# Seven tiles for the transposed adjacency block, with four five-chunk groups rotating through five of them

## The reference, cut to what matters

```
n, d = x.shape                      # 3327, 128
h = Wq.shape[0] // d                # 8
q = (x @ Wq.T).reshape(d, n, h)     # 128 heads
a = jnp.einsum('dnh,dmh->dnm', q, k) * scale
a = a + spatial_encoding + edge_encoding      # both are adj
a = jax.nn.softmax(a, axis=2)
out = jnp.einsum('dnm,dmh->dnh', a, v)
```

## The kernel before, in words

| group | steps | kind | size |
|---|---|---|---|
| 0 | 0, 1, 2, 5, 6 | summing | 2080 KB |
| 1 | 3, 4, 8, 12, 13 | product | 2080 KB |
| 2 | 7, 9, 10, 11, 14 | summing | 2080 KB |
| 3 | 15, 16, 18, 19, 20 | summing | 2080 KB |
| 4 | 22, 23, 24 | summing | 1248 KB |
| 5 | 17, 21, 25 | product | 1248 KB |

## Time and profile before

### The profile page before, as it was taken

How to read it: one execution, slowest core, us unless ns; L and a number is a source line. 1 busy time by engine, 2 the same in 40 slices (tenths; PEclk the granted TensorE clock), 3 DMA queues, 4 the chain that set the end, 5 groups by cost and what they waited for, 6 DMA issues and landing times. The chain is left out here.

```text
span 10714.4 us, 541771 instructions
## 1 busy us (share of the span) xinstructions
PE 10354.1 (97%) x216536; PEld 6775.6 (63%) x216536; DVE 9602.2 (90%) x10333; ACT 10168.5 (95%) x7764; POOL 8419.5 (79%) x4247
## 2 busy tenths in 40 slices
PE   8859999999999999999999999999999999999998
PEld 6626666666666666666666666666666666666666
DVE  7789999999998999999998999999998999999997
ACT  4459999999999999999999999999999999999997
POOL 4448888888887888888887888888887888888885
PEclk9989999999999999999999999999999999999999
DMA  7681111111112111111112111111112111111113
GB/s 226 204 272 43 42 42 42 42 42 42 42 42 83 42 43 42 43 42 43 42 42 81 42 42 42 42 42 42 42 42 81 42 42 42 42 42 42 42 42 89
DMA packets 579045, 652.59 MB, mean 61 GB/s; under 512 B 168827, under 2 KB 517914, under 8 KB 573114
## 3 DMA queue, kind: packets, MB, share of 16 engines
q1 hardware_dynamic: 577209, 622.77, 21.4%
HBM read 485.17 MB, written 137.18 MB: 58 GB/s over the span
## 5 line engine op out<-in xcount | busy, mean ns | idle before, releaser
L1137 DVE SCALAR_TENSOR_TENSOR at_sum<-attention_adj_t,at_score 128x832 f32<-128x832 f32 x9216 | 8808.9, 1016 | 883.7 <-PE at_score L1079 793.6
L1059 POOL TENSOR_TENSOR at_single<-at_single,attention_adj_t 128x832 f32<-128x832 f32 x4096 | 8083.9, 1997 | 1804.1 <-ACT at_single L1154 1767.3
L1157 ACT ACTIVATE at_sum<-at_sum 128x2496 f32<-128x2496 f32 x3072 | 7352.0, 2393 | 10.7 <-DVE at_sum L1137 10.7
L1079 PE MATMUL at_score<-attention_q,attention_k 128*32 128x512 bf16 (+1 forms) x106496 | 7193.4, 346 | 141.0 <-DVE at_sum L1137 61.1
L1079 PEld LDWEIGHTS at_score<-attention_q,attention_k 128*32 128x32 bf16 x106496 | 3607.0, 144 | 2238.3 <-DVE at_sum L1137 772.3
L1095 PE MATMUL at_acc<-at_sum,attention_v 128*9 128x208 f32 x73728 | 4848.5, 339 | 3.7 <-issue 2.7
L1154 ACT ACTIVATE at_single<-at_score 128x832 f32<-128x832 f32 x4096 | 3716.9, 957 | 40.9 <-PE at_score L1079 38.9
L1095 PEld LDWEIGHTS at_acc<-at_sum,attention_v 128*9 128x9 f32 x73728 | 1876.7, 91 | 904.0 <-issue 6.7
L1095 PE MATMUL at_acc<-at_single,attention_v 128*9 128x208 f32 x32768 | 2156.0, 339 | 0.0
L1095 PEld LDWEIGHTS at_acc<-at_single,attention_v 128*9 128x9 f32 x32768 | 834.6, 91 | 403.4 <-issue 1.5
L254 POOL TENSOR_TENSOR layer_col_acc<-layer_col_acc,st_a_rows 128x3328 f32<-128x3328 f32 x26 | 189.0, 7270 | 182.0 <-DMA st_a_rows<-in_adj_dram 182.0
(11 more groups left out here) (134 smaller groups left out, 1361.6 us busy)
## 6 DMA issues: line engine op xcount, KB each, us to landing
attention_k<-k_parts_scratch SPq DMA_DIRECT2D x1536, 156.0 KB
attention_q<-q_parts_scratch SPq DMA_DIRECT2D x4608, 13.0 KB
attention_v<-v_scratch SPq DMA_DIRECT2D x512, 112.5 KB
adj_t_scratch<-layer_a_t SPq DMA_DIRECT2D x26, 1664.0 KB, 7.6
st_a_rows<-in_adj_dram SPq DMA_DIRECT2D x25, 1663.5 KB, 9.2
attended_scratch<-at_o SPq DMA_DIRECT2D x1920, 7.3 KB
attention_adj_t<-adj_t_scratch SPq DMA_DIRECT2D x12, 2080.0 KB, 18.6
q_parts_scratch<-pr_partsq SPq DMA_DIRECT2D x39, 512.0 KB, 4.6
```

Of the source, the lines that this page charges most:

```text
L1059: pool.tensor_tensor(slot(n), slot(n), at[:, plan.chunk[n], :], ALU.mult).then_inc(multiplied, 1)
L1079: last = pe.matmul(score[plan.buffer(n)][32 * t:32 * (t + 1), a:b], keys[:, 32 * t:32 * (t + 1)], q[k][:, a:b], start=True, stop=True, til ...
L1137: dve.scalar_tensor_tensor(out=slot(n), in0=at[:, plan.chunk[n], :], scalar=2.0, in1=score[plan.buffer(n)][:, 0:NB], op0=ALU.mult, op1=ALU ...
L1157: act.activation(sums[buffer][:], sums[buffer][:], ACT.Exp).then_inc(exped, 1)
```

## The change

The one tile `adj_t` becomes seven: five of five chunks (`BIG_TILES`) and two of three chunks (`SMALL_TILE`). In all they hold 31 chunks, five more than a block has. The four groups of five chunks (0 to 3) are `big`; the two groups of three have a tile each for good. Group number `g` of block `b` lies in tile (4b + g) mod 5:

| block | group 0 | group 1 | group 2 | group 3 | free |
|---|---|---|---|---|---|
| 0 | 0 | 1 | 2 | 3 | 4 |
| 1 | 4 | 0 | 1 | 2 | 3 |
| 2 | 3 | 4 | 0 | 1 | 2 |
| 3 | 2 | 3 | 4 | 0 | 1 |

So group 0 of the next block (`leading`) has a tile that nobody reads in the present block, and SyncE loads it at the start of the present block, behind the store of the previous block's last head. At a block's end it loads groups 1 to 5 alone, each behind the last reader of its tile's `tenant`: group 1 waits for the old group 0 (step 6), group 2 for the old group 1 (step 13, a product), group 3 for the old group 2 (step 14), and groups 4 and 5 for their own predecessors (24 and 25). In `bound_scores` the buffer `amax` now lies in the fifth big tile, which is free at that time. The plan without products, which does not run here, gets other groups. `SOON` is not used.

The diff, cut to its core:

```diff
@@ load_group @@
-    sp.dma_start(at[:, first:first + count, :], src).then_inc(done, 16)
+    sp.dma_start(at[plan.tile_of(b, g)][:, 0:count, :], src).then_inc(done, 16)
@@ bound_scores @@
-        nq, nk, amax = s.sb("nq", [P, N]), s.sb("nk", [P, NP]), s.sb("amax", [P, N])
+        nq, nk = s.sb("nq", [P, N]), s.sb("nk", [P, NP])
+        amax = at[BIG_TILES - 1][:].rearrange("p c n -> p (c n)")[:, 0:N]
@@ Steps.__init__ @@
+        self.big = [g for g, steps in enumerate(self.groups) if len(steps) == CHUNKS_AT_ONCE]
+        self.small = [g for g in range(len(self.groups)) if g not in self.big]
+        self.shift = len(self.big) if products else 0
+        self.leading = self.big[:BIG_TILES - len(self.big)] if products else []
+        self.home = {n: (g, steps.index(n)) for g, steps in enumerate(self.groups) for n in steps}
@@ Steps @@
+    def tile_of(self, b, g):
+        if g in self.big:
+            return (self.shift * b + self.big.index(g)) % BIG_TILES
+        return BIG_TILES + self.small.index(g)
+
+    def tenant(self, b, g):
+        return next(((c, h) for c in range(b - 1, -1, -1) for h in range(len(self.groups))
+                     if self.tile_of(c, h) == self.tile_of(b, g)), None)
+
+    def adjacency(self, at, b, n):
+        g, place = self.home[n % C]
+        return at[self.tile_of(b, g)][:, place, :]
@@ load_adjacency @@
-                    last = plan.groups[g][-1]
-                    if b:
+                    tenant = plan.tenant(b, g)
+                    if tenant:
+                        then, last = tenant[0], plan.groups[tenant[1]][-1]
                         sp.wait_ge(multiplied if plan.is_product[last] else added,
-                                   plan.of_kind_before(b * BODIES - 1, STEPS - C + last + 1, plan.is_product[last]))
+                                   plan.of_kind_before((then + 1) * BODIES - 1, STEPS - C + last + 1, plan.is_product[last]))
                     load_group(sp, at_d, et_d, at, plan, g, b, at_loaded[g])
@@ attend, SyncE @@
                 for b in range(BLOCKS):
+                    for g in plan.leading if b + 1 < BLOCKS else []:
+                        sp.wait_ge(at_loaded[g], 16 * (b + 1))
+                        load_adjacency(b + 1, [g])
                     with sp.Fori(0, HEADS // 2 - 1) as i:
...
                             if k == 0:
-                                load_adjacency(b + 1, range(len(plan.groups)))
+                                load_adjacency(b + 1, [g for g in range(len(plan.groups)) if g not in plan.leading])
@@ attend, GpSimd and VectorE: the operand alone @@
-at[:, plan.chunk[n], :]
+plan.adjacency(at, b, n)
@@ gnn_two_layers @@
-            at = a.sb("adj_t", [P, C, NB])
+            at = [a.sb(f"adj_t{t}", [P, CHUNKS_AT_ONCE if t < BIG_TILES else SMALL_TILE, NB])
+                  for t in range(BIG_TILES + len(Steps(PRODUCTS).small))]
```

More of the change, by code:

```diff
@@ L52 @@
 CHUNKS_AT_ONCE = 5
+BIG_TILES = 5
+SMALL_TILE = 3
+SOON = 2
 PRODUCTS = 8
@@ L729, in _ @@
             dve.wait_ge(amax_loaded, 16)
-            dve.tensor_scalar(amax[:], amax[:], 2.0, None, ALU.mult).then_inc(steps, 1)
+            dve.tensor_scalar(amax, amax, 2.0, None, ALU.mult).then_inc(steps, 1)
             dve.wait_ge(nq_loaded, 16)
             chain.done()
-            dve.scalar_tensor_tensor(out=shift[:, 0:N], in0=nq[:], scalar=small[:, 0:1], in1=amax[:], op0=ALU.mult,
+            dve.scalar_tensor_tensor(out=shift[:, 0:N], in0=nq[:], scalar=small[:, 0:1], in1=amax, op0=ALU.mult,
                                      op1=ALU.add).then_inc(steps, 1)
@@ L901, in __init__ @@
             self.groups += [steps[m:m + CHUNKS_AT_ONCE] for m in range(0, len(steps), CHUNKS_AT_ONCE)]
+        if not products:
+            ends = (0, 5, 10, 15, 20, 23, 26)
+            self.groups = [list(range(a, b)) for a, b in zip(ends, ends[1:])]
         self.groups.sort(key=lambda steps: steps[-1])
         self.prefetched = [g for g, steps in enumerate(self.groups) if steps[0] < C // 3]
+        self.big = [g for g, steps in enumerate(self.groups) if len(steps) == CHUNKS_AT_ONCE]
[3 more added lines that the diff above has]
+        self.home = {n: (g, steps.index(n)) for g, steps in enumerate(self.groups) for n in steps}
         self.order = sorted(range(self.n), key=lambda n: (n // C, n + (self.LATE + 0.5) * self.is_product[n]))
@@ L1058, in _ @@
                                 pool.wait_ge(exped, plan.exped_by(i, n) + b * BODIES * UNITS)
-                                pool.tensor_tensor(slot(n), slot(n), at[:, plan.chunk[n], :],
+                                pool.tensor_tensor(slot(n), slot(n), plan.adjacency(at, b, n),
                                                    ALU.mult).then_inc(multiplied, 1)
@@ L1136, in _ @@
                                 dve.wait_ge(used, plan.used_by(i, plan.last_like(plan.slot, n)) + (b * BODIES * STEPS + AHEAD))
-                                dve.scalar_tensor_tensor(out=slot(n), in0=at[:, plan.chunk[n], :], scalar=2.0,
+                                dve.scalar_tensor_tensor(out=slot(n), in0=plan.adjacency(at, b, n), scalar=2.0,
                                                          in1=score[plan.buffer(n)][:, 0:NB], op0=ALU.mult, op1=ALU.add).then_inc(added, 1)
```

## The result

The changed kernel takes 10694.22 us (median of 20 runs, 10690.4 to 10700.42); the kernel before takes 10711.97 us beside it (20 runs). The ratio is 0.9983, 95% interval 0.9978 to 0.9989: 17.75 us faster, where 15.9 was forecast. Its profiled execution has a span of 10691.7 us against 10714.4.

A forecast was written before the change was run, and what follows sets the result against it. ScalarE's big exponentials were taken to bound the kernel, busy 95% of the span. One transfer less, 5.3 us at each of three boundaries, other edits 0: 10711.9 - 15.9 = 10696.0 us, range 10682 to 10708.

The forecast's parts named there:

- The size of the step: At each block boundary, group 0 leaves the DMA queue: 5.3 us gained, three times, 15.9 us in all.
- The first delay: Head 0 at a boundary: VectorE waits 5.2 us for group 2 before step 7; loss 5.9 us instead of 11.2.
- The second delay: Head 1's load at a boundary, queued behind the adjacency: TensorE still waits 2.1 us for its first weights.
- the rival with the larger gain: A: head 1's delay at the boundaries goes too, the clock perhaps helping; 24.6 us gained in all, chance 0.25.
- The edits costed at nothing: SyncE's tenant waits and the early group 0 load: cost 0; moved `amax`, operand addresses, seven tiles: 0, 2 us either way.
- A: Rival: head 1's load at the boundaries is no longer late; 24.6 us gained in all, chance 0.25.
- C: Rival, slower: early group 0 load delays head 2's load, 11.3 us each at three places, 18 us slower; chance 0.05.
- B: Rival: at the boundaries, empty DMA engines or late group 5 products leave 9 us gain; chance 0.10 together with D.
- D: Rival: group 0 not in place when the block begins, boundary cost unchanged, 10716 us; chance 0.10 together with B.

The follow-up runs named there:

- e10: The changed kernel itself, run again on the same chip as the repetition of e9: 10697.92 us, ratio 0.9988 to the kernel before.
- e1: Changed kernel with its tiles and rotation, but group 0 loaded at the boundary with the other five groups: 10721.24 us, ratio 1.0003 to the kernel before.
- e2: Kernel before with the adjacency reloads at the three boundaries left out: 10676.04 us beside 10718.08, ratio 0.9961.
- e5: Changed kernel with the loads of group 5 at the three boundaries left out: 10689.32 us, one run.
- e3: Kernel before with its one tile, group 0 issued ahead of head 0's load at a boundary: 10705.35 us beside 10718.08, ratio 0.9989.
- e7: Changed kernel with the early load of group 0 moved ahead of head 1's load at the first two boundaries: 10708.4 us, one run.
- e4: Changed kernel with group 1 issued ahead of head 0's load at a boundary: 10695.54 us beside 10718.08, ratio 0.9978.
- e6: Changed kernel with the loads of group 1 at the three boundaries left out: 10689.76 us, one run.
- e8: e4 with the loads of groups 4 and 5 at the boundaries left out: 10681.99 us, one run.
- e9: e4 with group 4 issued after the last head, ahead of head 1's load, and group 5 behind it: 10685.09 us, ratio 0.997; repeated, 10683.5 us.

## Why the prediction was right

*The size of the step.* One transfer of 2.13 MB fewer, 5.3 us at each boundary, 15.9 in all. Measured 4.7, 6.7 and 5.7, 17.1 in all. That the sum comes out so near is in part luck, since the single boundaries miss by 0.6 below and 1.4 above, and taken again (e10) the medians give 14.0 us instead of 17.75. e1 takes the early load away and loses everything; e2 finds the ceiling of 42 us that the result copies had given.

*The first delay.* Group 2 was to become the next thing that is late, with a wait of 5.2 us before step 7 and a copy 5.9 us late. At the third boundary it measured 5.03 us, and 8150.11 - 8125.34 = 24.77 us against 19.1: 5.7 us. Counted from the start of head 0's load (8124.33), group 2 came after 21.3 us; the forecast was 8160.1 - 8138.68 = 21.4. The order of landings carried over to a tenth.

*The second delay.* The forecast had TensorE wait 2.1 us for head 1's load at each boundary. It is 1.96 and 2.34 us at the first two, and the trace has none at the third; yet the third's second head also takes 1.9 us longer than usual. There the term is right in size by luck, and wrong in its cause. What held TensorE there is its clock. Windows at the third boundary, columns as above:

```profile
8144.00:8146.00 2.00, 0.00 (x0) 0.00 (x0) 0.36 (x1) 0.00 (x0) 2.00 (x2) 0.95 1.00 389
8146.00:8148.00 2.00, 1.28 (x16) 0.69 (x20) 1.81 (x3) 1.30 (x1) 0.06 (x1) 0.50 1.03 404
8148.00:8150.00 2.00, 2.00 (x28) 0.88 (x24) 1.63 (x2) 0.98 (x1) 0.00 (x0) 0.50 1.03 404
8150.00:8152.00 2.00, 2.00 (x32) 0.94 (x28) 0.47 (x2) 0.93 (x2) 0.52 (x1) 0.50 1.03 401
8152.00:8154.00 2.00, 2.00 (x44) 1.23 (x40) 0.87 (x1) 2.00 (x2) 2.00 (x2) 0.84 1.02 398
```

After the stop of 4.66 us the granted clock is 0.50 (1.2 GHz) until past 8152. Four steps start 1.39 us apart there (8146.72, 8148.12, 8149.51, 8150.89) where they later take 0.70: 2.8 us lost behind a stop of 4.66. At the first boundary the half clock lasts 5.5 us and costs 2.7, at the second 3.9 and 1.7. The forecast had seen the half clock and hung it on the rival with the larger gain, instead of giving it a term. It is one: stop and clock together, 4.66 + 2.8 = 7.5 us, are what the third boundary takes over the undisturbed pair (7.6), and in e5, with head 1's wait away, 4.53 + 2.3 = 6.8 us at the third boundary are what is left there (6.8). At the first two boundaries of the changed kernel TensorE's stops (1.34, 3.49 and 1.96; 4.70 and 2.34) and the clock add up to 9.5 and 8.7 us, of which 9.2 and 8.4 show. Why head 1's load is late by 2 us at two boundaries and not at the third stays open. Only the first two have the early load behind it, but e3, which has none, waits 2.45, 2.50 and 1.56 us, so that alone does not explain it.

*The edits costed at nothing.* SyncE's waits for the tenants held nothing up: group 1 was there for GpSimd at 8140.29, 16.0 us after head 0's load began, forecast 16.2. GpSimd had waited 2.48 us for it by then, at the other two boundaries up to 3.2 and 3.7, and no stop of TensorE is put down to that. The early load took 0.88 us of issue in the first block and 0.40 in the others. In the third block it was issued at 5701.87 and landed 10.4 us later, at 5712.3, and head 2's load began at 5716.63: 4.4 us of room, where 4 were reckoned.

*The rivals.* A (the second delay goes too) had its condition fulfilled at the third boundary, where head 1's load was in time, and gave nothing, since the half clock took its place; e7 shows that the load does stand behind what is queued. C (slower, by the early load in a head load's way) has its mechanism confirmed by e7, 6.0 us at a boundary, in the place where the change didn't put it; its price of 11.3 us was not tried. B's late group 5 is small: GpSimd waits 12.9 us in all, less than before. D is excluded by the waits.

## What to carry to other kernels

Where a resident block is replaced, ask what is queued ahead of the first late reader and ahead of the small loads behind it: the price is bytes by rate, and a second buffer helps only by what it moves out of that queue. Look first whether the DMA engines stand empty just before it; one issue moved there gave nearly what five chunks of memory gave at the boundaries. A transfer removed is worth its full time only while its successor in the queue is the bound: after it came a half clock, a head load and a loop's jump, each taking its share.

## What the runs showed of the hardware

- TensorE stood 3.07 to 3.53 us at the jump back of its loop when it reached it at full speed with the DMA engines at 1.0 of their time (e4, e6, six boundaries). With the engines drained (e8, and e9 with its repetition, nine boundaries) it stood 0.28 to 0.86 us there. The profile calls the long stop "issue". A packet of 16 KB of the instruction queue starts 2.7 to 2.8 us before each long stop ends.
- After stops of 3.5 to 4.9 us TensorE ran 3.8 to 5.6 us at 1.2 GHz (granted clock 0.50), which cost 1.6 to 2.8 us on top (the three boundaries of the changed kernel, the third of the kernel before, the third of e5). The stops of about 3 us at the jump were followed by a lower clock as well (0.62 and 0.53 in e4's windows from 8152 to 8156), while the clock stayed at 1.00 behind e8's stop of 1.35 us at 8131.9.
- Small head loads on the queue of SyncE came late by about the time of a transfer issued ahead of them (e7: 2.13 MB, TensorE's wait 5.7 and 4.8 us longer, two heads 6.0 us longer).
- While the DMA engines were at 1.0 of their time, SyncE was held 5.41 and 5.98 us in issuing the fourth and fifth group at the third boundary of the kernel before, where the first three took 0.40 to 0.52 us, and the loads moved at 393 to 413 GB/s.
